# A new order for one PSUM bank: moving the front of a Mamba and expert block by half slots

## The reference, cut to what matters

```python
xn = layernorm(x)
# Mamba block: 256 inner channels, 16 states, convolution over 4 tokens
xi, z = split((rmsnorm(xn) * rms_w) @ in_proj)
xi = silu(conv(xi) + conv_b)
dt, B, C = split(xi @ x_proj)
delta = softplus(dt @ dt_w + dt_b)
h = exp(delta * A) * h + delta * xi * B      # a scan over the tokens
y = (sum(h * C) + xi * D) * silu(z)
mamba = xn + y @ out_proj
# experts: probabilities, a gate that keeps the top 80%, eight small networks
gate = probs * keep(softmax(xn @ Wr + br))
ffn = sum over e of gate[e] * (relu(xn @ W1[e] + b1[e]) @ W2[e] + b2[e])
x = x + mamba + ffn
```

## Time and profile before

| | |
|---|---|
| median of 3 runs | 2105.19 us (2105.03 to 2108.21) |
| the profiled execution | 2106.87 us |
| its span | 2105.0 us |
| mean granted clock of TensorE | 0.957 |
| busy share of the span | PE 91%, DVE 80%, ACT 64%, POOL 62% |

### The profile page before, as it was taken

One profiled execution on the slowest core, in us unless ns is written; L12 is line 12 of the kernel. 1 busy time (PEld: TensorE's weight loads), 2 busy tenths in 40 slices (PEclk: granted clock), 3 DMA queues, 4 the chain that ended last, 5 costly groups with the idle time before them and its releaser, 6 DMA issues. The chain is left out here.

```text
span 2105.0 us, 39182 instructions
## 1 busy us (share of the span) xinstructions
PE 1905.6 (91%) x14386; PEld 1117.0 (53%) x14386; DVE 1680.0 (80%) x2731; ACT 1337.3 (64%) x2423; POOL 1308.6 (62%) x1005
## 2 busy tenths in 40 slices
PE   5789999999999999999999999994899999998984
PEld 3445555555555555555555555553455555554542
DVE  5588889898888887988989879884888777776655
ACT  3577776776777767767777677651455555554652
POOL 2577877868778788688787787863433333333660
PEclk7899999999999999999999999995899999998997
DMA  8633615425336154263360632606444444445558
GB/s 201 154 85 72 140 42 122 106 47 145 80 78 141 34 130 101 52 141 78 86 139 24 141 90 57 141 6 169 118 124 112 115 118 118 117 135 144 176 142 243
DMA packets 211994, 234.89 MB, mean 112 GB/s; under 512 B 31590, under 2 KB 150414, under 8 KB 207694
## 3 DMA queue, kind: packets, MB, share of 16 engines
q1 hardware_dynamic: 207116, 227.98, 43.3%
q0 software_dynamic: 2048, 4.18, 0.7%
q10 hardware_dynamic: 2640, 0.24, 0.1%
HBM read 165.51 MB, written 66.85 MB: 110 GB/s over the span
## 5 line engine op out<-in xcount | busy, mean ns | idle before, releaser
L731 POOL TENSOR_TENSOR dBx<-REP,BC 128x1024 f32<-128x1024 f32 x256 | 603.8, 2362 | 251.8 <-DVE dA L904 221.8
L904 DVE TENSOR_TENSOR_SCAN dA<-dA,dBx 128x512 f32<-128x512 f32 x512 | 626.1, 1223 | 154.3 <-POOL dBx L731 105.9
L403 PE MATMUL UP<-xnT,W 128*128 128x512 f32 x1024 | 517.3, 622 | 51.0 <-ACT hT L605 45.4
L412 PEld LDWEIGHTS DN<-W,hT 128*128 128x128 f32 x4096 | 469.5, 192 | 97.7 <-issue 67.8
L412 PE MATMUL DN<-W,hT 128*128 128x128 f32 x4096 | 495.1, 278 | 0.3 <-ACT GD L612 0.3
L596 ACT ACTIVATE dA<-REP,A 128x512 f32<-128x512 f32 x512 | 354.1, 695 | 88.1 <-DVE PR L913 80.5
L605 ACT ACTIVATE hT<-UP,b 128x512 f32<-128x512 f32 x512 | 355.4, 694 | 67.1 <-PE UP L403 61.6
L913 DVE TENSOR_TENSOR PR<-dA,BC 128x512 f32<-128x512 f32 x512 | 353.6, 691 | 16.0
L403 PEld LDWEIGHTS UP<-xnT,W 128*128 128x128 f32 x1024 | 179.1, 194 | 288.7 <-issue 163.6
L1808 DVE TENSOR_REDUCE NM<-S 128x4 f32<-128x1024 f32 (+1 forms) x192 | 234.1, 1219 | 78.1 <-PE S L1353 77.9
L1567 ACT ACTIVATE PT<-S 128x1024 f32<-128x1024 f32 x192 | 197.2, 1027 | 93.7 <-PE S L1353 93.6
(11 more groups left out here) (251 smaller groups left out, 2648.7 us busy)
## 6 DMA issues: line engine op xcount, KB each, us to landing
BC<-s_b SPq DMA_DIRECT2D x128, 256.0 KB, 5.8
REP<-s_dx SPq DMA_DIRECT2D x124, 256.0 KB, 7.4
REP<-s_delta SPq DMA_DIRECT2D x124, 256.0 KB, 8.8
s_parts<-SPL SPq DMA_DIRECT2D x64, 192.0 KB
KS<-s_parts SPq DMA_DIRECT2D x64, 192.0 KB
QS<-s_parts SPq DMA_DIRECT2D x64, 192.0 KB
s_dx<-tz SPq DMA_DIRECT2D x16, 512.0 KB, 3.1
s_y<-zeros SPq DMA_DIRECT2D x32, 256.0 KB, 2.8
```

Source lines behind the costliest of these rows:

```text
L403: nc.tensor.matmul(UP[k % 2][:], W1[:, e % E0, f * P:(f + 1) * P], xnT[:, q, :], start=True, stop=True).then_inc(upf.sem, 1)
L412: last = nc.tensor.matmul(DN[:, j * P:(j + 1) * P], hT[:, e % 2, f, j * P:(j + 1) * P], W2[:, e, f, :], start=(f == 0), stop=(f == FB - 1))
L731: nc.gpsimd.tensor_tensor(dBx[:, s % 2], DX[:, h, j:j + 2, :], BC[:, q // 2, q % 2, :].unsqueeze(1).to_broadcast([P, 2, T0]), ALU.mult).th ...
L904: nc.vector.tensor_tensor_scan(h, h, dBx[:, k // 2 % 2, k % 2, :], 0.0, ALU.mult, ALU.add).then_inc(scan_done.sem, 1)
```

## The change

It moves steps of the front. The convolution's steps, xproj and all up to exp stand two or four half slots earlier; the transposes of XN (xnt) come right after the convolution; z1 comes ahead of z0; the gate is no longer transposed at the end of the block before, but in half slot 16 of its own block, as a part of `slot`; XN's and XQ's steps on POOL stand at half slots 13, 15 and 17 of the block before, so EARLY is 19. The tanh of z has a buffer of its own, where it shared xch. Waits follow the new order of the bank.

```diff
-    xrT = sb("xrT", [P, T0]); dtB = sb("dtB", [P, T0])
+    xrT = sb("xrT", [P, T0]); tanhz = sb("tanhz", [P, T0]); dtB = sb("dtB", [P, T0])
-    umax, lnw, one_w, tanhz = xch, th, tz, xch
+    umax, lnw, one_w = xch, th, tz
-    front = signal("front", 11)
+    front = signal("front", 10); turned = signal("turned", 1)
-    NORMS_AT, ROOTS_AT = (8, 12, 15), (9, 13)
+    NORMS_AT, ROOTS_AT = (6, 9, 12), (7, 10)
-    EARLY = 7
-    PE_AT = dict(xqt=-2, x0=0, x1=4, out=8, xproj=10, dt0=12, dt1=16, xnt=17, logits=19, z0=23, z1=27, gt=29)
-    ACT_AT = dict(xr=-2, tap0=2, tap1=4, tanh=6, dtb=10, d0=14, d1=16, xn=18, exp=17, one=17, ln=18, gexp=20, tz0=23, tz1=27, gt=29)
-    DVE_AT = dict(conv0=3, conv1=5, xi=8, soft=19, lg=19, lnw=20, gate1=23, z0=25, gate2=27, z1=29, ev1=3, store=9, stat=12, ev0=21)
-    POOL_AT = dict(xm=-7, xq=-4, xs=-4, ff=10, r=20, dx=23, rank=23, yz1=3, yz0=22, delta=20, lg=21, keep=27)
+    EARLY = 19
+    PE_AT = dict(xqt=-6, x0=-4, x1=0, xnt=4, out=6, xproj=8, dt0=10, dt1=14, gt=16, logits=18, z1=20, z0=23)
+    ACT_AT = dict(xr=-6, tap0=-2, tap1=0, tanh=2, xn=4, dtb=8, d0=10, d1=14, exp=15, one=16, gt=17, ln=18, gexp=20, tz1=22, tz0=24)
+    DVE_AT = dict(conv0=-1, conv1=1, xi=4, soft=17, lg=19, lnw=20, gate1=23, z1=23, z0=25, gate2=27, ev1=3, store=7, stat=11, ev0=21)
+    POOL_AT = dict(xm=-19, xq=-17, xs=-15, ff=9, r=18, dx=23, rank=23, yz1=3, yz0=22, delta=20, lg=21, keep=27)
-    SP_AT = dict(bst=11, dst=15, est=23, bc0=26, save=10, load=12)
+    SP_AT = dict(bst=9, dst=15, est=23, bc0=26, save=8, load=10)
...
     def slot(h, it, par, ...):                       # PE
-                    output(it - 1, 1 - par, lambda: pe.wait_ge(conv_step.sem, conv_step.at(it + 1, 6)))
+                    output(it - 1, 1 - par, lambda: pe.wait_ge(xT_copied.sem, xT_copied.at(it + 1, 2)))
+            if h == PE_AT["gt"]:
+                pe.wait_ge(gate_made.sem, gate_made.at(it, 5))
+                if final:
+                    pe.wait_ge(x_done.sem, x_done.at(it - 1, 1))
+                else:
+                    pe.wait_ge(u_done.sem, u_done.at(it + 1, 2))
+                nc.tensor.transpose(FRO[0:J0 * E0, 0:P], gate[:, par].rearrange("p j e -> p (j e)"), ident[:]).then_inc(turned.sem, 1)
...
     def fore(h, n, q):                               # PE
             if h == PE_AT["xqt"]:
-                pe.wait_ge(gT_copied.sem, gT_copied.at(n - 1, 1))
+                pe.wait_ge(z_done.sem, z_done.at(n - 1, 2))
             if h == PE_AT["xproj"]:
-                pe.wait_ge(conv_step.sem, conv_step.at(n, 6))
+                pe.wait_ge(xT_copied.sem, xT_copied.at(n, 2))
             if h == PE_AT["xnt"]:
-                pe.wait_ge(u_done.sem, u_done.at(n, 2))
+                pe.wait_ge(conv_step.sem, conv_step.at(n, 6))
             if h == PE_AT["logits"]:
-                pe.wait_ge(xT_copied.sem, xT_copied.at(n, 2))
+                pe.wait_ge(u_done.sem, u_done.at(n, 2))
+                pe.wait_ge(gT_copied.sem, gT_copied.at(n - 1, 1))
+            if h == PE_AT["z1"]:
+                pe.wait_ge(gate_step.sem, gate_step.at(n, 1))
+            if h == PE_AT["z0"]:
+                if bank(n, 1) is FRO:
+                    pe.wait_ge(z_done.sem, z_done.at(n, 1))
...
     def fore(h, n, q):                               # ACT
                     if k == 0:
-                        act.wait_ge(z_done.sem, z_done.at(n - 1, 2))
+                        act.wait_ge(delta_done.sem, delta_done.at(n - 1, 1))
...
     def fore(h, n, q):                               # POOL, xm
-                pool.wait_ge(front.sem, front.at(n - 1, 7))
+                pool.wait_ge(front.sem, front.at(n - 1, 4))
...
     def fore(h, n, q):                               # DVE
+            if h == DVE_AT["z1"]:
+                dve.wait_ge(tanh_z.sem, tanh_z.at(n, 1))
+                dve.wait_ge(yz_done.sem, yz_done.at(n - 2, 2))
+                nc.vector.scalar_tensor_tensor(z1[:, q, :], tanhz[:], 1.0, bank(n, 1)[:], ALU.add, ALU.mult).then_inc(z_done.sem, 1)
```

More of the change, by code:

```diff
@@ L372, in _ @@
     def _(pe):
-        for s in (front, upf, downf, sumf, outf):
+        for s in (front, turned, upf, downf, sumf, outf):
             pe.sem_inc(s.sem, 2 * s.per)
@@ L513, in fore @@
                 last.then_inc(front.sem, 1)
[L514 to L526, removed]
+            if h == PE_AT["z1"]:
+                pe.wait_ge(gate_step.sem, gate_step.at(n, 1))
+                nc.tensor.matmul(bank(n, 1)[:], inproj[:, 3 * P:4 * P], xrT[:], start=True, stop=True).then_inc(front.sem, 1)
+            if h == PE_AT["z0"]:
+                if bank(n, 1) is FRO:
+                    pe.wait_ge(z_done.sem, z_done.at(n, 1))
+                nc.tensor.matmul(FRO[:], inproj[:, 2 * P:3 * P], xrT[:], start=True, stop=True).then_inc(front.sem, 1)
         def between(s):
@@ L534, in end @@
             add_states(HALF * NQ - 1, it)
-            output(it, par, lambda: pe.wait_ge(x_done.sem, x_done.at(it - 1, 1)))
+            output(it, par, lambda: pe.wait_ge(gT_copied.sem, gT_copied.at(it, 1)))
         pipeline(fore, start, slot, end, pe, between)
@@ L634, in slot @@
                 apply_gate(s // 2, it, par)
+            if h == ACT_AT["gt"]:
+                act.wait_ge(outf.sem, outf.at(it - 2, 1))
+                act.wait_ge(turned.sem, turned.at(it, 1))
+                nc.scalar.copy(gT[:, par, :], FRO[0:J0 * E0, 0:P]).then_inc(gT_copied.sem, 1)
             if first and h in ROOTS_AT:
@@ L638, in delta_input @@
         def delta_input(k, n):
-            act.wait_ge(front.sem, front.at(n, 5 + k))
+            act.wait_ge(front.sem, front.at(n, 6 + k))
             nc.scalar.activation(umax[:, k, :], bank(n, k)[:], ACT.Relu, bias=dtb[:, k:k + 1])
@@ L661, in fore @@
             if h == ACT_AT["dtb"]:
-                act.wait_ge(front.sem, front.at(n, 4))
+                act.wait_ge(front.sem, front.at(n, 5))
                 act.wait_ge(b_stored.sem, b_stored.at(n - 1, 16))
@@ L676, in fore @@
                 act.wait_ge(upf.sem, upf.at(n - 2, E0 * FB))
-                act.wait_ge(front.sem, front.at(n, 7))
+                act.wait_ge(front.sem, front.at(n, 4))
                 nc.scalar.copy(xnT[:, q, :], FRO[:]).then_inc(xT_copied.sem, 1)
@@ L696, in fore @@
                 if h == ACT_AT[f"tz{k}"]:
[L698 to L705, removed]
+                    act.wait_ge(z_done.sem, z_done.at(n, 0 if k else 1))
+                    act.wait_ge(front.sem, front.at(n, 10 - k))
+                    nc.scalar.activation(tanhz[:], bank(n, k)[:], ACT.Tanh, scale=0.5).then_inc(tanh_z.sem, 1)
         pipeline(fore, start, slot, lambda it, par: None, act, between)
@@ L745, in times_z @@
             pool.wait_ge(ev_done.sem, ev_done.at(it, h + 1))
-            pool.wait_ge(z_done.sem, z_done.at(it, h + 1))
+            pool.wait_ge(z_done.sem, z_done.at(it, 2 - h))
             nc.gpsimd.tensor_tensor(y[:, h, :], y[:, h, :], z0[:] if h == 0 else z1[:, par, :], ALU.mult).then_inc(yz_done.sem, 1)
@@ L994, in fore @@
                 nc.vector.reciprocal(g4[:, 2, :], g4[:, 1, :]).then_inc(gate_step.sem, 1)
+            if h == DVE_AT["z1"]:
+                dve.wait_ge(tanh_z.sem, tanh_z.at(n, 1))
+                dve.wait_ge(yz_done.sem, yz_done.at(n - 2, 2))
+                nc.vector.scalar_tensor_tensor(z1[:, q, :], tanhz[:], 1.0, bank(n, 1)[:], ALU.add, ALU.mult).then_inc(z_done.sem, 1)
             if h == DVE_AT["z0"]:
-                dve.wait_ge(tanh_z.sem, tanh_z.at(n, 1))
+                dve.wait_ge(tanh_z.sem, tanh_z.at(n, 2))
                 dve.wait_ge(yz_done.sem, yz_done.at(n - 1, 1))
-                nc.vector.scalar_tensor_tensor(z0[:], tanhz[:, 0, :], 1.0, FRO[:], ALU.add, ALU.mult).then_inc(z_done.sem, 1)
+                nc.vector.scalar_tensor_tensor(z0[:], tanhz[:], 1.0, FRO[:], ALU.add, ALU.mult).then_inc(z_done.sem, 1)
             if h == DVE_AT["gate2"]:
@@ L1004, in fore @@
                 nc.vector.tensor_reduce(cum[:], eq[:], AX.X, ALU.add).then_inc(gate_step.sem, 1)
[L1005 to L1009, removed]
         pipeline(fore, lambda: None, slot, end, dve, between)
```

2 lines of the change are left out of this document (1 added, 1 removed).

## The result

The changed kernel takes 2133.96 us, median of 4 runs (2132.55 to 2137.6), beside 2106.7 for the kernel before on the same chip: ratio 1.0129, 95% interval 1.0117 to 1.0141. It is slower, as forecast, by 27 us in place of 18. The profiled execution took 2137.6 us.

What follows compares the result with a forecast made beforehand. The prediction took a ring of waits across ACT, DVE, POOL and PE as the bound: 0.84 us more in each of 14 blocks (12) plus 6 at the start, 18 us, gives 2123 against the median; own range 2111 to 2133, wide 2096 to 2138.

Steps and rivals of the forecast that it cites:

- a ring over ACT, DVE, POOL and DVE: Chain of waits across engines, then PE to the next block, said to set the block: 84.97 us against 84.13.
- D to `one`: ACT's stretch from the block's first UP product of half slot 16 (moment D) to the step one: 5.16 us.
- soft to lnw: DVE's stretch from soft, with three scans and their products, to lnw's end: 8.34 us, ending at D + 13.50.
- delta to scan 26: POOL's stretch from delta to the end of dBx 13, handovers included, which scan 26 awaits: 15.69 us.
- scan 26 to conv0's end: DVE's stretch through gate2 and the wait for POOL's keep and dBx 15: 14.58 us, x1 at D + 43.8.
- on to half slot 5: DVE and ACT from conv0's end to the second UP pair of half slot 5: 11.42 us, holding PE again.
- PE to the next D: PE's own work from half slot 5 to the next block's first UP product of half slot 16: 29.78 us.
- The clock: PE's granted clock, read as 1.00 in the 84 us profiled, so nothing was to be had from it.
- The start: Before the first scan, POOL's delta of block 0 waits behind block 1's XI load: 6 us lost, range 3 to 9.
- Rival 1: PE is the bound, with its first pair in after conv0 ends: 2.0 us less a block, 2083 us, chance 0.19.
- Rival 2: DVE's soft keeps 2.11 us or more beside POOL's accumulation: 0.9 more a block, 2136 us, chance 0.12.
- Rival 3: The change does nothing that counts; conv0 comes 0.5 us a block sooner than thought: about 2104 us, chance 0.11.

Runs made afterwards that it cites:

- e1: Changed kernel with XI of block 1 loaded ahead of the x tiles and last weights: 2121.99 us, ratio 1.0068 to the kernel before.
- e8: Changed kernel with DVE's xi one half slot later (4 to 5): 2132.62 us, ratio 1.0123 to the kernel before.
- e10: Changed kernel with XI loaded early, soft 18, exp 16, rank 24, B and C loads at 22, keep 28: 2070.78 us, ratio 0.9830 to the kernel before.
- e7: Changed kernel with XI of block 1 loaded early, soft at 18, exp at 16 and rank at 24: 2105.2 us, ratio 0.9987 to the kernel before.
- e4: Changed kernel with XI of block 1 loaded early and soft at half slot 18: 2112.45 us, ratio 1.0014 to the kernel before.
- e11: Kernel before the change, with POOL's rank 23 to 24 and B and C loads 26 to 22: 2093.21 us, ratio 0.9937.
- e3: Changed kernel with tap0 and conv0 one half slot earlier: 2158.82 us, ratio 1.0237 to the kernel before.
- e5: Changed kernel with POOL's rank 23 to 24, behind dBx 13: 2128.17 us, ratio 1.0100 to the kernel before.

## Why the prediction was right, and where not

**The direction and its mechanism** held: a ring over ACT, DVE, POOL and DVE, in which a wait at x1 takes the place of the one at the gate. The terms, from the rows of after, in the order of the prediction: D to `one` 4.99 (5.16 forecast); soft to lnw 8.31 (8.34); delta to scan 26 15.70 (15.69); scan 26 to conv0's end 14.72 (14.58), so x1 at D + 43.72 (43.8); on to half slot 5 11.51 (11.42), D + 55.23 (55.2).

**PE to the next D** was mis-sized: 29.78 forecast, 30.37 measured (782.06 to 812.43). The half pair costs 1.05 (782.06 to 783.11), not 0.90. DN split by dt1 costs 1.98 + 1.89, 3.87 in place of 3.68 (807.51 to 809.49, 810.54 to 812.43). The two pairs at 802.30 take 4.21, not 4.05. Together 0.50 of the 0.59. Why the same products cost more in these places is not shown.

**The block it is held against** was another error, of the other sign: the forecast compared with one block of 84.13, but thirteen blocks before average 84.64. The 45 us of PE without a gap behind the gate, too, are that block's: eight of thirteen have a wait at x1. So 84.97 against 84.13 gave +0.84, and 85.66 against 84.64 gives +1.02. The difference was nearly right by luck: two errors of 0.5 to 0.7 cancel. The 14 blocks cost 14.3, not 12.

**The clock** was read in one stretch. That nothing is to be had from it holds for the earlier trace rows, but in seven of thirteen blocks before it falls at the 2.60 wait. The new order ends that, which the forecast does not count. What it is worth here cannot be told apart from the waits for DVE, which are shorter behind a fall.

**The start** was forecast at 6 within 3.4 to 9, and e1 shows 8.0, nearer to the worst bound. Delta went to memory 6.2 later, not 6.8 (64.86 for 58.69); the rest lies behind it, up to tap0 and conv0 ahead of the first scan.

**Layer 1** was not in the forecast at all. The blocks' 14.3 leave 8.9 of layer 0's 23.2 for the start and the two blocks at the ends; e1 shows 8.0 of them. The profiled pair has 7.7 more in layer 1 (687.0 after its last store, 679.3 before), and the median's 27 some 4. The clock's rows above account for the profiled pair: 88 matmuls fewer are some 7 us at full clock, where 50 us hold about 600. For the medians, of which only one execution is profiled, it is argued and not shown.

**Costed at nothing.** Xi's longer time (2.37 in place of 1.21) was foreseen, and said to be free; e8, where another 0.57 costs nothing, bears that out. The gate's transpose waits for nothing in its new place, as forecast. XI's load in the steady blocks: POOL's XN at half slot 13 waits for nothing.

**The rivals.** Rival 1 (PE is the bound, 2083) wasn't the case here, but e10, with six edits to the ring and the start, comes near what it would have been: a block of 82.28 and 2071. The prediction's 80.4 for PE's own work is not reached; a wait of 1.02 is left. Rival 2's mechanism is real (lnw in e7, xi here), only not at soft, where POOL was free: its 1.23 beside a POOL that waits is what the Trainium skill, "SBUF — State Buffer", section "Who interferes with whom", leads one to expect, and e8's pair of rows shows the rest of that rule, that whichever of the two came first holds the other up until it is through. Rival 3's sum has a sign wrong: conv0 0.5 sooner leaves a block 0.34 longer, and with the start's 6 that is 2116, not 2104.

**The signs named ahead** came out: 1.49 at x1 (above 1), soft at D + 5.0, scan 26's wait 3.55 (above 3), first scan at 83.88 (after 80). The time, 2133.96, lies a microsecond above the forecast's own range (2111 to 2133) and inside the wide one.

## What to carry to other kernels

When an order is changed in a kernel whose fullest engine is 95% busy, follow one turn of the ring across engines: it gave five of six terms within 0.2 us here, where busy shares gave nothing. Look at each small step that stands ahead of a large one in the same list without being wanted soon (rank and keep ahead of dBx, dx's loads ahead of B and C): moving the three gave most of what e10 gained over e4 (2.54 us a block, exp's move among them), and rank's move alone had given 0.31: each paid only when the path beside it was shortened too. Measure the block over all blocks, not from one, and look at the granted clock in each of them: a mean of 0.98 over a block can hide a fall to 0.50.

## What the runs showed of the hardware

Two instructions of DVE and POOL can hold each other up to the end: xi took 2.94 beside a dBx, and the accumulation behind it 2.26 in place of 1.28. DVE's products PR have two inputs as well, but one of them, dA, lies in PSUM and only BC in SBUF. All 425 of them between 200 and 1340 us in the changed kernel took 675 to 693 ns, and 168 of these had a dBx beside them for nine tenths of their time or more: an instruction with one input in SBUF pays nothing here.

TensorE's granted clock fell from 1.00 to 0.50 inside layer 0, at or just behind waits of PE: of 2.60 (seven of thirteen blocks before), 2.61 (seven of thirteen in e11), 2.98 (nine of thirteen in e3), 1.86 and 1.79 (e7), 1.42 (once in e8). In e11 such a block is 1.7 us longer. Which waits are followed by a fall is not shown: one of 2.07 in e5 is not.

The granted clock of PE rises to full at another time in layer 1 from one execution to the next (in the second 50 us after layer 0), and the rest of the span follows: 0.64 with 687.0 us in the changed kernel, 0.74 with 685.0 in e4, 0.86 with 679.3 before, 0.87 with 677.5 in e10. The runs of one kernel spread by nearly as much: e4's twelve lie at 2106.6 to 2114.9.
